# Last combination of a two-layer kernel: part of the gate product and of the additions moved from VectorE to GpSimd, and the first load of rows split in two

## The reference, cut to what matters

```python
# _L1_ffn_ref: 8 experts, the two best of each token, weights normalised to sum 1
for e in range(NUM_EXPERTS):
    hid = jax.nn.silu(x @ w1[e].T) * (x @ w3[e].T)
    out = out + hid @ w2[e].T * gates[:, e:e + 1]
...
x = x + gb * _L1_ffn_ref(h, ...)      # gb: one row of 128 numbers per batch
return x
```

## Time and profile before

| | us |
|---|---|
| three runs | 586.12, 587.73, 588.39 |
| median | 587.73 |
| profiled execution, span from first to last instruction | 586.0 |
| GpSimd's last scatter starts | 567.31 |
| first load of rows is issued | 569.65 |
| ScalarE's first product of the combination starts | 572.98 |
| VectorE's last addition starts | 582.90 |

### The profile page before, as it was taken

The page is one execution under the profiler, slowest core; times in us unless marked ns, Lnnn a source line. Parts: engine busy times, 40 slices in busy tenths (PEclk is TensorE's granted clock), DMA queues, the critical chain, the costliest instruction groups (busy, mean ns, idle before and its releaser), DMA issues.

```text
span 586.0 us, 13132 instructions
## 1 busy us (share of the span) xinstructions
PE 526.7 (90%) x4044; PEld 374.2 (64%) x4044; DVE 424.8 (72%) x1662; ACT 328.6 (56%) x544; POOL 315.5 (54%) x478
## 2 busy tenths in 40 slices
PE   5989979967489999999999999999998899999960
PEld 5667769965157445444444454445577799999960
DVE  4776736735859899999999999996678454454436
ACT  3854426632573477777777777776630544444423
POOL 3441154417644486566686668666710677777630
PEclk9999989998699899999999999999999899999995
DMA  8500112221671546647634653433850111111115
GB/s 317 221 2 19 55 35 71 71 70 52 126 145 24 122 104 129 126 108 169 153 88 110 154 135 72 93 91 66 299 151 19 45 48 51 49 49 51 43 37 204
DMA packets 90498, 58.21 MB, mean 99 GB/s; under 512 B 72674, under 2 KB 76771, under 8 KB 88615
## 3 DMA queue, kind: packets, MB, share of 16 engines
q1 hardware_dynamic: 81550, 41.18, 28.0%
q0 software_dynamic: 3744, 7.68, 5.1%
q10 hardware_dynamic: 5136, 8.52, 4.1%
HBM read 37.72 MB, written 19.63 MB: 98 GB/s over the span
## 4 chain that ended last, share of the span: by engine, by line
PE 76%; DVE 12%; DMA 4%; issue 3%; ACT 3%; POOL 2%; SPq 0%; ACTq 0%; POOLq 0%; DVEq 0%
PE banks L1167 15%; PE banks L2021 13%; PE banks L2009 12%; PE banks L1995 11%; PE banks L1180 9%; DVE banks L1718 2%; PE banks L1961 1%; PE banks L1154 1%; PE banks L765 1%; DMA f_hg<-scratch_h_rows,r_source 1%; PE banks L366 1%; DMA a_at<-scratch_back_rows,home 1%; PE banks L2109 1%; DVE f_upd L1080 1%; DVE a_rest_ L1637 1%
## 5 line engine op out<-in xcount | busy, mean ns | idle before, releaser
L1718 DVE CUSTOM_DVE_ANT_1 banks<-banks,a_mask 128x480 f32<-128x480 f32 (+14 forms) x480 | 190.0, 459 | 14.7 <-PE banks L1995 12.9
L1867 ACT ACTIVATE a_prob_<-banks 128x1024 f32<-128x1024 f32 x160 | 154.1, 1021 | 48.7 <-PE banks L2009 48.7
L1534 POOL TENSOR_SCALAR_AFFINE_SELECT a_prob_<-a_prob_ 128x512 f32<-128x512 f32 x128 | 80.8, 635 | 67.0 <-ACT a_prob_ L1867 67.0
L1995 PEld LDWEIGHTS banks<-a_k_u_,a_q_u_ 72*128 72x128 bf16 x512 | 64.9, 148 | 64.5 <-DVE a_neg_max_ L1718 31.1
L1995 PE MATMUL banks<-a_k_u_,a_q_u_ 72*128 72x512 bf16 (+15 forms) x512 | 102.4, 291 | 2.4 <-DVE a_neg_max_ L1718 2.4
L1167 PE MATMUL banks<-f_hgt,f_w_now 128*112 128x128 f32 (+1 forms) x808 | 101.2, 277 | 0.0
L2009 PE MATMUL banks<-a_q_u_,a_k_x_ 75*128 75x512 bf16 x320 | 97.4, 386 | 0.4 <-ACT a_prob_ L1867 0.4
L1167 PEld LDWEIGHTS banks<-f_hgt,f_w_now 128*112 128x112 f32 (+1 forms) x808 | 95.6, 184 | 0.0
L978 POOL DMA_INDIRECT f_hg<-scratch_h_rows,r_source x62 | 59.6, 962 | 61.2 <-DVE r_source L299 31.6
L2021 PE MATMUL banks<-a_prob_,a_v_g_ 128*32 128x512 f32 (+3 forms) x1024 | 83.5, 444 | 0.4 <-POOL a_prob_ L1534 0.4
L1718 DVE DVE_READ_ACCUMULATOR2_ANT a_neg_max_<- 128x1 f32 x512 | 72.3, 143 | 0.0
(11 more groups left out here) (247 smaller groups left out, 714.1 us busy)
## 6 DMA issues: line engine op xcount, KB each, us to landing
a_q_u_<-scratch_q_parts SPq DMA_DIRECT2D x15, 576.0 KB
scratch_o_rows<-a_o_sb_ ACTq DMA_DIRECT2D x28, 256.0 KB, 2.2
w<-in_w SPq DMA_DIRECT2D x2, 2048.0 KB, 10.5
w<-in_w SPq DMA_DIRECT2D x2, 1792.0 KB, 12.3
scratch_q_parts<-a_part_ SPq DMA_DIRECT2D x24, 128.0 KB
a_k_u_<-scratch_k_parts SPq DMA_DIRECT2D x48, 48.0 KB
f_back<-scratch_back_rows SPq DMA_DIRECT2D x4, 512.0 KB, 4.7
w<-in_w SPq DMA_DIRECT2D x2, 896.0 KB, 19.6
```

The lines of the kernel that those rows point to most:

```text
L1534: nc.gpsimd.affine_select(out=block_p, in_=block_p, pattern=[[0, JH], [1, P]], compare_op=ALU.is_ge, fill=0.0, base=0, channel_multiplier= ...
L1718: last = nc.vector.tensor_tensor_reduce(out=found, in0=found, in1=mask[:, :, TG - 4 * (t + 1):], scale=-1.0, scalar=-MASKED, op0=ALU.add, ...
L1867: nc.scalar.activation(prob[g % 2][:, 2 * e:2 * e + 2].rearrange("p s j t c -> p (s j) t c"), PS[:, b0:b0 + 2, :].rearrange("p s (j c t) - ...
L1995: last = nc.tensor.matmul(PS[:, a % 3, off:off + width], queries[:, g % 2, :, t], k_u[r][:, :, g % 2 * TG:g % 2 * TG + 4 * (t + 1)], start ...
```

## The change

Four edits, all in the second layer's part of `experts_programs`:

1. GpSimd gets, behind its last scatter, the gate product of batch 0 and the final additions of batches 0, 1 and 2. It waits for VectorE (`summed`) once per batch, and between the product and the addition of batch 0 for itself (`pool_step`).
2. VectorE keeps all sixteen additions of `y1`, the gate products of batches 1, 2 and 3, and the final addition of batch 3.
3. The load of batch 0 comes as two of 256 KB, tokens 0 and 1 of each partition first (2 KB per partition each), with a semaphore of its own (`half_in`). ScalarE and VectorE wait for the first before token 0 and for the second before token 2. SyncE so issues five loads in place of four.
4. SyncE waits for GpSimd's additions before the outputs of batches 0 to 2, and for VectorE's before that of batch 3.

```diff
@@ sync
+            back_rows_in(0, slice(0, NI // 2), half_in)
+            back_rows_in(0, slice(NI // 2, NI), back_in[0])
+            for b in range(1, B):
+                back_rows_in(b, slice(0, NI), back_in[b])
             for b in range(B):
-                sp.wait_ge(x_ready, b + 1)
+                if b < B - 1:
+                    sp.wait_ge(pool_step, b + 2)
+                else:
+                    sp.wait_ge(x_ready, 1)
                 sp.dma_start(dram["out"][b]...
@@ gpsimd
             scatter(S - 2)
             scatter(S - 1)
+            for b in range(B - 1):
+                ub, xb = upd[:, b * NI:(b + 1) * NI, :], x_sb[:, b * NI:(b + 1) * NI, :]
+                gp.wait_ge(summed, b + 1)
+                if b == 0:
+                    nc.gpsimd.tensor_tensor(ub, ub, sb["gates"][:, b, layer, 1, :].unsqueeze(1).to_broadcast([P, NI, D]), ALU.mult
+                                            ).then_inc(pool_step, 1)
+                    gp.wait_ge(pool_step, 1)
+                nc.gpsimd.tensor_tensor(xb, xb, ub, ALU.add).then_inc(pool_step, 1)
@@ vector
             for t in range(b * NI, (b + 1) * NI):
+                if t == 0:
+                    ve.wait_ge(half_in, 16)
+                if t == NI // 2 or (b and t == b * NI):
+                    ve.wait_ge(back_in[b], 16)
                 ve.wait_ge(first_choice, t + 1)
...
+            if b == 0:
+                last.then_inc(summed, 1)
+                continue
             ch.wait()
...
+            gated = nc.vector.tensor_tensor(ub, ub, gb.unsqueeze(1).to_broadcast([P, NI, D]), ALU.mult)
+            if b < B - 1:
+                gated.then_inc(summed, 1)
+            else:
+                ch.link(gated)
+                nc.vector.tensor_tensor(xb, xb, ub, ALU.add).then_inc(x_ready, 1)
```

More of the change, by code:

```diff
@@ L942, in experts_programs @@
     back_in = [semaphore(f"f_back_in{b}_") for b in range(B)] if layer else None
+    summed, pool_step = (semaphore("f_summed"), semaphore("f_pool_step")) if layer else (None, None)
+    half_in = semaphore("f_half_in") if layer else None
     def w_first(e):
@@ L961, in sync, with back_rows_in @@
                 sp.wait_ge(y_out[q], 16 * ((S - 1 - q) // YR + 1))
-            for b in range(B):
[L964 to L967, removed]
-                sp.wait_ge(x_ready, b + 1)
+            def back_rows_in(b, tokens, landed):
+                sp.dma_start(back[:, b * NI + tokens.start:b * NI + tokens.stop, :, :],
+                             back_rows[b * T * K:(b + 1) * T * K, :].rearrange("(p i k) d -> p i k d", p=P, k=K)[:, tokens]
+                             ).then_inc(landed, 16)
+            back_rows_in(0, slice(0, NI // 2), half_in)
+            back_rows_in(0, slice(NI // 2, NI), back_in[0])
+            for b in range(1, B):
+                back_rows_in(b, slice(0, NI), back_in[b])
+            for b in range(B):
+                if b < B - 1:
+                    sp.wait_ge(pool_step, b + 2)
+                else:
+                    sp.wait_ge(x_ready, 1)
                 sp.dma_start(dram["out"][b].rearrange("(p i) d -> p i d", i=NI),
@@ L1075, in vector @@
         for b in range(B if layer else 0):
-            ve.wait_ge(back_in[b], 16)
             gb = sb["gates"][:, b, layer, 1, :]
             for t in range(b * NI, (b + 1) * NI):
+                if t == 0:
+                    ve.wait_ge(half_in, 16)
+                if t == NI // 2 or (b and t == b * NI):
+                    ve.wait_ge(back_in[b], 16)
                 ve.wait_ge(first_choice, t + 1)
-                ch.step(nc.vector.scalar_tensor_tensor(upd[:, t, :], back[:, t, 1, :], gate[:, 1, t:t + 1],
-                                                       upd[:, t, :], ALU.mult, ALU.add))
+                last = nc.vector.scalar_tensor_tensor(upd[:, t, :], back[:, t, 1, :], gate[:, 1, t:t + 1],
+                                                      upd[:, t, :], ALU.mult, ALU.add)
+                if b or t < NI - 1:
+                    ch.step(last)
+            if b == 0:
+                last.then_inc(summed, 1)
+                continue
             ch.wait()
             ub, xb = upd[:, b * NI:(b + 1) * NI, :], x_sb[:, b * NI:(b + 1) * NI, :]
-            ch.link(nc.vector.tensor_tensor(ub, ub, gb.unsqueeze(1).to_broadcast([P, NI, D]), ALU.mult))
-            nc.vector.tensor_tensor(xb, xb, ub, ALU.add).then_inc(x_ready, 1)
+            gated = nc.vector.tensor_tensor(ub, ub, gb.unsqueeze(1).to_broadcast([P, NI, D]), ALU.mult)
[4 more added lines that the diff above has]
+                nc.vector.tensor_tensor(xb, xb, ub, ALU.add).then_inc(x_ready, 1)
         if layer:
-            ve.wait_ge(x_ready, B)
+            ve.wait_ge(x_ready, 1)
     def scalar(ac):
@@ L1140, in scalar @@
             for b in range(B):
-                ac.wait_ge(back_in[b], 16)
                 for t in range(b * NI, (b + 1) * NI):
+                    if t == 0:
+                        ac.wait_ge(half_in, 16)
+                    if t == NI // 2 or (b and t == b * NI):
+                        ac.wait_ge(back_in[b], 16)
                     nc.scalar.activation(upd[:, t, :], back[:, t, 0, :], ACT.Copy, scale=gate[:, 0, t:t + 1]
```

## The result

The changed kernel takes 591.36 us (median of 6 runs, 590.73 to 593.15) against 587.28 us for the kernel before (6 runs, 585.78 to 588.39). The ratio is 1.0081, with a 95% interval of 1.0062 to 1.0100: slower by 0.8%, some 4 to 5 us. The forecast was 588.8 us with a range up to 590.4 us, and slower by over 0.5% had a chance of 0.10. The forecast was wrong.

The account below looks back on a forecast made before the run. VectorE's list bounds the tail: 2.9 us moved and 0.6 by the split, against 0.68, 0.56 and three times 1.08 us of waiting, end 1.05 us later; 587.73 + 1.05 = 588.8 us, range 588.0 to 589.8, 8 in 10 585.8 to 590.4.

Parts of the forecast that it names:

- Turn-taking: Second layer's tail: GpSimd and VectorE instructions with two SBUF inputs exclude each other, 1.08 us per GpSimd addition, three times.
- VectorE's list between turns: Batches 1 and 2 on VectorE: additions of y1 and gate product 1.77 us, plus one GpSimd instruction 1.08 us.
- The rival that GpSimd and VectorE overlap: Tail: these instructions don't exclude each other, VectorE ends 2.75 us earlier, 585.0 us; whole or partial overlap, chance 0.11.
- the one that GpSimd stretches: Tail: GpSimd works slowly while holding its turn, 1.27 us becomes 2.03, 3.04 us more, 591.8 us; chance 0.06.
- a hold to the recorded end: Tail: GpSimd keeps VectorE out for its whole 1.27 us, an end 0.70 us later than the forecast's.
- The split: Batch 0's load in two halves: VectorE finishes batch 0 at 574.05 instead of 574.64, a gain of 0.59 us.
- what the fifth issue does to later loads: SyncE's extra load issue: 0.43 us on batch 1's load, hidden by what follows.
- Everything else costs nothing: End of GpSimd's list and SyncE's issues: no cost beyond VectorE's terms; last output issued 2.41 us before the span's end.

Follow-up runs that it names:

- the useless additions: The kernel before plus a GpSimd DRAIN behind its last scatter and three 128x512 GpSimd additions nobody needs: 589.77 us, ratio 1.0040.
- the early DRAIN: The changed kernel plus a DRAIN of GpSimd right behind its last scatter, ahead of its new work: 589.88 us, ratio 1.0036.
- the late clearing: The kernel before plus one GpSimd clearing of 128x4 numbers after VectorE's final addition of batch 2: 589.99 us, ratio 1.0048.

## Why the prediction was wrong

*Turn-taking: right.* Each of batches 1, 2 and 3 had one long addition of y1, the first 0.99 us and the others 1.35. The range of the sixteen is in one row:

```profile
L1101 DVE SCALAR_TENSOR_TENSOR f_upd<-f_back,f_gate,f_upd x16: 336/344/1348, 571.1 to 581.6; 128x128 f32<-128x128 f32 x16
```

A GpSimd addition beside a full VectorE cost 1.348 - 0.344 = 1.00 us, where 1.08 was forecast. VectorE's list between turns was right: batch 2's first addition of y1 to batch 3's took 2.78 us (577.07 to 579.85), forecast 1.77 + 1.08 = 2.85. The rival that GpSimd and VectorE overlap is refuted by this and by the useless additions, and so is the one that GpSimd stretches: its rows are 1.25 to 1.30 us, by themselves. VectorE got in 0.19 us before the recorded end of GpSimd's 1.30 us, where the prediction took 0.13; a hold to the recorded end would have been those 0.19 us too long per addition.

*The split: mis-sized, with the wrong sign.* Forecast: a gain of 0.59 us and an untouched batch 1. The first half did come early (2.83 from the issue, forecast 2.65), and batch 0 was ready at 5.01 (forecast 4.40). But batch 1's rows were 1.7 us later. I had bounded what the fifth issue does to later loads by its 0.43 us, from rows of undisturbed loads. VectorE could first use a turn for batch 1 at 7.49 instead of 5.63. It got back 1.08 there, because the first addition of GpSimd fell into that wait, which the forecast had paid as a turn among batch 1's additions (the rows were there at 6.35, VectorE ready at 6.85, and GpSimd's addition kept it out until 7.49); and 0.14 in the turns that followed. 1.86 - 1.08 - 0.14 = 0.64, and 1.05 + 0.64 is the measured 1.69 us. With the load whole again VectorE's end was the same within 0.06 us, and with the split alone it was 1.07 us later than before: in no run did the split bring its 0.59 us.

*The failed step: "Everything else costs nothing: GpSimd's waits stand behind its last scatter with nothing behind them but these instructions".* Something did stand behind them, GpSimd's closing DRAIN, and it cost 5.9 - 2.4 = 3.5 us, twice the loss of VectorE. It was in the trace of before, in the closing line's own rows. The description of the kernel before, "nothing of GpSimd follows them", has the same hole. The prediction asked what GpSimd's work does to VectorE and to the outputs, and closed GpSimd's list at its last visible instruction. Without it the 1.69 us of VectorE would put the kernel near 589.0 us, inside the range; that is worked out and not run. The nearest runs pay or hide the DRAIN but differ in VectorE's part too: with batch 0 alone on GpSimd 1.4 us slower than before (VectorE 0.84 later), with the early DRAIN 0.36%, 2.1 us (VectorE 2.8 later).

Added up from the first load's issue: 1.69 + 3.47 = 5.2 us by one profiled execution, against 0.81% of 587, 4.8 us, by the runs. Runs bear out that the DRAIN is the larger part, not the two numbers themselves: the late clearing, which moves the DRAIN alone, costs 0.48%, and the changed work with the DRAIN out of the way 0.24% and 0.36%.

That the time came near the stretching rival's 591.8 us is chance; its mechanism did not happen.

No version beats the kernel before. While VectorE has work with two SBUF inputs, an addition moved to GpSimd takes 0.6 us off its list and puts 1.0 us of waiting on it; the kernels that differ from before by the split alone are at 0.9996 to 1.0008 of it.

## What to carry to other kernels

An engine's list ends with its share of the program's closing, not with its last visible instruction. Before work is put at the end of an engine that was done early, ask the trace for the closing line's rows and add the engine's DRAIN behind the new last instruction; if it is long, an explicit DRAIN in an idle stretch pays it in advance, as long as nothing waits for that engine meanwhile (here it held GpSimd until 6.4 us from the issue). And moving a two-input SBUF operation from VectorE to GpSimd did not pay here while VectorE had two-input SBUF work of its own to do: each took 0.6 us off and put 1.0 us on.

## What the runs showed of the hardware

- GpSimd's DRAIN ended 7.75 to 7.77 us after its last instruction at the end of a program with 117 indirect DMAs from GpSimd, whatever that instruction was (a scatter, a 1.30 us addition, a 0.10 us clearing that began 12.8 us behind the last scatter's end). With another DRAIN between scatters and last instruction it ended within 0.1 us of that instruction, or took 0.04 us. With a DRAIN ahead of the last 78 of them, that one ended 1.40 us and the closing one 6.44 us after the instruction in front; the other engines' closing DRAINs took 0.01 to 2.1 us.
- GpSimd's 1.27 us clearing cost VectorE's two-input instructions nothing (0.34 us throughout). Its addition of 1.07 us cost them 0.79 us, the one of 1.30 us 1.00 us.
- A GpSimd addition of 128x512 with one tensor as both inputs took 1.07 us, with two tensors 1.26 to 1.30 us; no run parts this from the other differences between them.
- One load of four cut in two, the bytes unchanged, put a pause of the stream, up to about 2 us long, on a batch that could not wait, where it had fallen on one that could.
